# Two tiles a body, loaded row by row by SyncE, each with 25 of the empty places, and a new order of the first steps

## What is computed

```python
z = jnp.concatenate([x[dst], x[src], edge_attr], axis=-1)
msg = jax.nn.sigmoid(z @ Wf + bf) * jax.nn.softplus(z @ Ws + bs)
summed = jax.ops.segment_sum(msg, dst, num_segments=n)
cnt = jax.ops.segment_sum(jnp.ones((dst.shape[0],), x.dtype), dst, num_segments=n)
out = summed / jnp.maximum(cnt, 1.0)[:, None]
out = (out - rmean) * jax.lax.rsqrt(rvar + BN_EPS) * gamma + beta
return out + x
```

## Time and profile before

| | |
|---|---|
| median of the runs | 2086.69 us |
| the profiled execution | 2085.8 us, of which 2084.0 us span |
| busy: DVE, ACT, PE, POOL | 84%, 78%, 74%, 71% of the span |
| POOL's gathers, L402 | 1498 from the table, 56 of plain rows |
| SP's single rows, L330 | 1792 (14 tiles of 128) |
| mean TensorE clock granted | 0.94 of full |
| DMA | 339 MB, 163 GB/s in the mean |

### The profile page before, as it was taken

How to read it: one execution, slowest core, us unless ns; L and a number is a source line. 1 busy time by engine, 2 the same in 40 slices (tenths; PEclk the granted TensorE clock), 3 DMA queues, 4 the chain that set the end, 5 groups by cost and what they waited for, 6 DMA issues and landing times. The chain is left out here.

```text
span 2084.0 us, 41078 instructions
## 1 busy us (share of the span) xinstructions
PE 1540.8 (74%) x8321; PEld 1266.5 (61%) x8321; DVE 1745.7 (84%) x3574; ACT 1618.0 (78%) x3692; POOL 1481.8 (71%) x1575
## 2 busy tenths in 40 slices
PE   7777777777677777777587777777777777777773
PEld 6666666656556666565466566566665555666652
DVE  6799988989889889798638999798788887988887
ACT  5699887878778778688457889698787777877884
POOL 6577777777777777777267777777777777777770
PEclk9999999999999999999799999899899999999995
DMA  8455555555555555555475555555555555555552
GB/s 293 119 169 161 169 171 158 159 161 168 161 159 158 170 159 158 161 166 162 134 230 152 171 167 170 151 168 164 156 168 161 165 161 158 161 161 167 159 148 62
DMA packets 168890, 339.48 MB, mean 163 GB/s; under 512 B 62702, under 2 KB 93030, under 8 KB 168643
## 3 DMA queue, kind: packets, MB, share of 16 engines
q0 software_dynamic: 73824, 200.29, 32.4%
q1 hardware_dynamic: 93298, 135.27, 21.7%
q10 hardware_dynamic: 1522, 1.72, 0.3%
HBM read 315.49 MB, written 19.81 MB: 161 GB/s over the span
## 5 line engine op out<-in xcount | busy, mean ns | idle before, releaser
L402 POOL DMA_INDIRECT pre<-s_rows,ends x1498 | 1417.8, 946 | 482.9 <-issue 445.8
L516 PE MATMUL pre_ps<-rhs,lhs 128*128 128x256 f32 x3136 | 832.7, 409 | 450.5 <-DVE lhs L774 449.8
L516 PEld LDWEIGHTS pre_ps<-rhs,lhs 128*128 128x128 f32 x3136 | 592.6, 199 | 667.6 <-DVE lhs L774 418.8
L798 DVE TENSOR_TENSOR pre<-pre_ps,pre 128x1024 f32<-128x1024 f32 x378 | 460.6, 1219 | 50.5 <-DMA pre<-s_rows,ends 50.5
L609 ACT ACTIVATE logs<-pre 128x512 f32<-128x512 f32 x392 | 246.9, 630 | 306.6 <-DVE pre L798 265.9
L774 DVE SCALAR_TENSOR_TENSOR lhs<-lhs,base_f,sum_ps 64x256 f32<-64x256 int32 x784 | 373.3, 476 | 114.7 <-issue 51.8
L531 PEld LDWEIGHTS sum_ps<-hot,msg 128*128 128x128 f32 x3136 | 435.1, 201 | 55.9 <-issue 25.0
L531 PE MATMUL sum_ps<-hot,msg 128*128 128x64 f32 x3136 | 414.3, 278 | 29.6 <-DVE sums L817 19.4
L603 ACT COPY rhs<-dst_ps 64x256 f32<-64x256 f32 x792 | 290.0, 366 | 62.6 <-issue 31.3
L809 DVE TENSOR_TENSOR msg<-soft_ps,logs 128x512 f32<-128x512 f32 x392 | 271.0, 691 | 13.3
L802 DVE SCALAR_TENSOR_TENSOR soft_ps<-soft_ps,pre 128x512 f32<-128x512 f32 x392 | 270.4, 690 | 1.1 <-ACT soft_ps L616 1.0
(11 more groups left out here) (92 smaller groups left out, 573.7 us busy)
## 6 DMA issues: line engine op xcount, KB each, us to landing
lhs<-dge_and_destination_cols SPq DMA_DIRECT2D x196, 512.0 KB
single<-s_rows SPq DMA_DIRECT2D x1792, 1.0 KB
pre<-s_rows,ends POOLq DMA_INDIRECT x1498, 2.8
s_rows<-logs SPq DMA_DIRECT2D x8, 512.0 KB, 7.3
s_rows<-x_t SPq DMA_DIRECT2D x7, 512.0 KB, 12.0
s_rows<-msg SPq DMA_DIRECT2D x6, 512.0 KB, 7.0
x_rows<-pre SPq DMA_DIRECT2D x12, 256.0 KB
out<-y_out SPq DMA_DIRECT2D x12, 256.0 KB, 2.3
```

Of the source, the lines that this page charges most:

```text
L402: nc.gpsimd.indirect_dma_start(pre[:, slot(k, j), i, 0:width], None, rows, bass.IndirectOffsetOnAxis(ap=ends[:, k, j * TILES + i, 0:1], ax ...
L516: ins = nc.tensor.matmul(pre_ps[:, j % 2, i, :], lhs[:, j // 2, edges], rhs[:, j, i // 2, :], start=True, stop=not plain(b, k, j))
L798: nc.vector.tensor_tensor(rows, pre_ps[:, j % 2], rows, ALU.add).then_inc(s_pre[j], 1)
```

## The change

- `SINGLES = ((3, 3), (6, 3))`: two tiles a body, the last tiles of steps 15 and 27, are left to SP. Each of the 28 such tiles of the program (14 a layer) holds only 103 edges (`SINGLE_ROWS`): its last 25 places are empty. 14 x 25 = 350 of the 352 empty places are moved there from the end of the list, by the host's arrangement of the inputs.
- SP issues 206 single rows a body where it issued 128, in all 14 halves, 13 to 17 in each (7 in the last; `CUT`), where it was 12 in each of 11. `single` and `sp_src` have two places. The list of the first tile is read during the body before; that of the second in halves 1 and 3. The first tile is put in place at the start of half 7, after the last of its rows landed, the second at the end of half 13.
- POOL gathers 110 tiles a body where it gathered 111.
- Layer 1's stages come in another order: `hot`, `logs`, `msg`, then five in `x1_t`, of which stores 10 to 12 use the first three again. ACT waits for the flag of sortedness before double 10, not before the first.
- The four memsets of the counts go from DVE to POOL, ahead of its wait for the stores.
- DVE makes `one_hot` of steps 1 to 3 right after `hot_transposed`. PE's `turn` is called at the end of the step before.
- DVE clears `single` once a layer (the 25 empty rows are never written after).

```diff
-SINGLE = (BODY - 1, SLOTS - 1, TILES - 1)
-SINGLE_ROWS = 12
+SINGLES = ((3, 3), (6, 3))
+SINGLE_ROWS = 103
+CUT = ((0, 13, 30, 43, 60, 73, 90, 103), (0, 17, 32, 49, 64, 81, 96, 103))
...
-            s_stage = in_x1[0:3] + s_stage[0:2] + s_stage[4:5] + s_stage[2:4] + in_x1[3:5]
+            s_stage = s_stage[4:5] + s_stage[0:4] + in_x1
...
+        place = lambda c: (c if c < len(s_stage) else c - len(in_x1)) if first else c % len(s_stage)
+        stores_of = lambda r, c=STORES: 16 * sum(place(e) == r for e in range(c))
...
+            def load_singles(i, part):
+                rows = range(CUT[i][part], CUT[i][part + 1])
+                at_row = nc.values_load_multi_w_load_instructions(
+                    sp_src[:, i, rows[0]:rows[-1] + 1], engines=[ENG.SP], min_val=0, max_val=NPAD - 1,
+                    skip_runtime_bounds_check_because="sources are rows of the table")[1]
+                for p, r in zip(rows, at_row):
+                    sp.dma_start(single[p:p + 1, i, :], s_dram[bass.ds(r, 1), :]).then_inc(singles_in, 16)
+
+            def place_singles(i, b):
+                k, j = SINGLES[i]
+                sp.wait_ge(singles_in, b * (32 * SINGLE_ROWS) + (i + 1) * (16 * SINGLE_ROWS))
+                sp.sem_inc(passed, 1)
+                done(sp, s_soft, group_no(b, k), j, RING)
+                sp.sem_inc(passed, 1)
+                sp.dma_start(pre[:, slot(k, j), TILES - 1, :], single[:, i, :]).then_inc(single_in, 16)
+
+            def singles(b, half):
+                if half == 0:
+                    sp.wait_ge(list_in, b * 64 + 32)
...
+                if half == BODY:
+                    sp.wait_ge(list_in, b * 64 + 64)
+                    sp.sem_inc(passed, 1)
+                    place_singles(0, b)
+                load_singles(half // BODY, half % BODY)
+                if half == 1:
+                    load_block(group_no(b, SINGLES[1][0]))
+                if half == 3:
+                    load_list(1, b * 64 + 48)
+                if half == BODY + 2:
+                    load_block(group_no(b, SINGLES[0][0]) + BODY)
+                if half == BODY + 4:
+                    load_list(0, b * 64 + 80)
                 if half == 2 * BODY - 1:
-                    place_singles(b, group_no(b, SINGLE[0]))
+                    sp.wait_ge(single_in, b * 32 + 16)
+                    sp.sem_inc(passed, 1)
+                    place_singles(1, b)
...
+                        if first:
+                            for c in range(4):
+                                cols = slice(c * (NPAD // 4), (c + 1) * (NPAD // 4))
+                                nc.gpsimd.memset(t["sums"][:, 1, cols], 0.0).then_inc(zeroed, 1)
...
-                    gather(s_dram, F2, k, j, TILES - ((k, j) == SINGLE[0:2]))
+                    gather(s_dram, F2, k, j, TILES - ((k, j) in SINGLES))
...
-                    if plain(b, k, j):
-                        turn(SLOTS * k + j)
-                    else:
+                    if not plain(b, k, j):
                         product(b, k, j)
...
                     if plain(b, k, j):
                         product(b, k, j)
+                        if SLOTS * k + j + 1 < PLAIN:
+                            turn(SLOTS * k + j + 1)
...
-                if c >= len(s_stage) and i % 2 == 0:
-                    act.wait_ge(s_out[r], 16 * (c // len(s_stage)))
+                if stores_of(r, c) and i % 2 == 0:
+                    act.wait_ge(s_out[r], stores_of(r, c))
...
-                if live(0) and four_back:
+                if live(0) and (four_back or SLOTS * k + j):
                     one_hot(g, k, j)
```

More of the change, by code:

```diff
@@ L214, in store_rows @@
             sp.dma_start(dram[c * 4 * P:(c * 4 + n) * P, :].rearrange("(w p) f -> p w f", p=P),
-                         stage[c % len(stage)][:, 0:n, :]).then_inc(out[c % len(stage)], 16)
+                         stage[place(c)][:, 0:n, :]).then_inc(out[place(c)], 16)
         @block.sync
@@ L320, in load_singles @@
                         for r in range(len(s_stage)):
-                            sp.wait_ge(s_out[r], 16 * len(range(r, STORES, len(s_stage))))
+                            sp.wait_ge(s_out[r], stores_of(r))
                     else:
-                        sp.wait_ge(single_in, b * 16)
+                        sp.wait_ge(single_in, b * 32)
                         sp.sem_inc(passed, 1)
[L325 to L338, removed]
@@ L348, in one @@
+            load_block(SINGLES[0][0])
+            load_list(0, 16)
             def one(b, k):
@@ L373, in _ @@
             sp.wait_ge(sp_tab_in, groups * 16 + 16)
+            sp.wait_ge(list_in, bodies * 64 + 32)
             sp.sem_inc(passed, 1)
@@ L646, in one @@
                     step = SLOTS * k + j - 3
-                    if first and isinstance(b, int) and step in (0, 12):
-                        for r in ((0, 1, 2) if step == 0 else (8, 9)):
-                            act.wait_ge(s_out[r], stores_of(r))
+                    if first and isinstance(b, int) and step in range(0, 4 * len(in_x1), 4):
+                        act.wait_ge(s_out[5 + step // 4], stores_of(5 + step // 4))
                     if first and isinstance(b, int) and 0 <= step < DOUBLES:
@@ L789, in sums @@
                 done(v, s_prod, g, j, 0)
-                single = (k, j) == SINGLE[0:2]
-                v.wait_ge(src_in[k][j], turn * (16 * (TILES - single)))
-                if single:
-                    v.wait_ge(single_in, turn * 16)
+                if (k, j) in SINGLES:
+                    v.wait_ge(src_in[k][j], turn * (16 * (TILES - 1)))
+                    v.wait_ge(single_in, turn * 32 + 16 * (SINGLES.index((k, j)) - 1))
+                else:
+                    v.wait_ge(src_in[k][j], turn * (16 * TILES))
                 rows = pre[:, slot(k, j), :, 0:F2]
@@ L860, in stages @@
                 step = SLOTS * k + j
-                if first and isinstance(b, int) and step < 4:
-                    nc.vector.memset(t["sums"][:, 1, step * (NPAD // 4):(step + 1) * (NPAD // 4)], 0.0).then_inc(zeroed, 1)
                 if isinstance(b, int) and step == 0:
                     v.wait_ge(s_out[hot_stage], stores_of(hot_stage))
-                if live(0) and not four_back:
+                if live(0) and not four_back and step == 0:
                     one_hot(g, k, j)
@@ L1067 @@
     x_t[:, :NODES] = a["x"].T
-    dst = np.full((EPAD + P,), NO_NODE, a["dst"].dtype)
-    dst[:EDGES] = a["dst"]
+    short = np.array([(g * SLOTS + j) * TILES + TILES - 1 for g in range(GROUPS) for k, j in SINGLES if g % BODY == k])
+    used = np.ones((EPAD // P, P), bool)
+    used[short, SINGLE_ROWS:] = False
+    place = np.flatnonzero(used)[:EDGES]
+    last = np.arange(PAIR - 1, EPAD, PAIR)
+    last[short // (TILES // PAIRS)] -= P - SINGLE_ROWS
+    in_order = np.full((EPAD + P,), NO_NODE, a["dst"].dtype)
+    in_order[:EDGES] = a["dst"]
+    dst = np.full((EPAD,), NO_NODE, a["dst"].dtype)
+    dst[place] = a["dst"]
     ends = np.zeros((EPAD, 2), a["src"].dtype)
-    ends[:EDGES, 0] = a["src"]
-    ends[:, 1] = dst[:EPAD]
+    ends[place, 0] = a["src"]
+    ends[:, 1] = dst
     features = np.zeros((FE, EPAD), a["edge_attr_64"].dtype)
-    features[:, :EDGES] = a["edge_attr_64"].T
+    features[:, place] = a["edge_attr_64"].T
     features = features.reshape(FE, EPAD // STEP, PAIRS, PAIR)
-    ends_row = dst[:EPAD].view(features.dtype).reshape(EPAD // STEP, PAIRS, PAIR)
+    ends_row = dst.view(features.dtype).reshape(EPAD // STEP, PAIRS, PAIR)
     edge_cols = np.empty((P, EPAD // STEP, PAIRS, PAIR), features.dtype)
```

60 lines of the change are left out of this document (27 added, 33 removed).

## The result

The kernel became slower: 2432.7 us in the median of four runs (2429.81 to 2434.64) against 2086.3 for the kernel before beside it (2085.7 to 2089.22). The ratio is 1.1656, interval [1.1636, 1.1676]. The direction was as forecast, the size wasn't: 2172 us was forecast and 2225 was the top of the range. The rise is 346 us where 86 were expected, four times as much.

The account below looks back on a forecast made before the run. POOL was taken as the bound before the change, SyncE after: 100.1 + 32.4 + 5.2 + 2.3 + 0.8 + 2.7 = 143.5 us a body; 2084.0 + 45.4 + 40.9 plus 1.8 around gave 2172 us, range 2100 to 2225.

Parts of the forecast that it names:

- What bounds the kernel now: In the loop before the change, POOL sets the pace at 1.250 us a gather; SyncE has some 39 us to spare.
- POOL, 17.5 us: POOL's 7 fewer gathers a layer save 17.5 us; its body falls from 138.8 to 137.5 us.
- SyncE, more rows, 32.4 us a body: On SyncE's queue, 78 more rows a body at 0.415 us each add 32.4 us.
- SyncE, register reads, +5.2 us (bounds 0.9 to 9): SyncE's reads of row numbers into registers grow from 10.2 to 15.4 us a body, bounds 0.9 to 9 more.
- The second list and the placement, 2.3 and 0.8: On SyncE, loading a second list adds 2.3 us a body and placing a second tile 0.8.
- Waits for landing, 2.7 us a body (bounds 0 to 5): SyncE's two waits a body for the tiles' last rows to land add 2.7 us, bounds 0 and 5.
- First bodies: At layer starts, step 4's edge load issues at 68 us behind 30 rows; second bodies begin 16.2 and 8.5 us later.
- Ends of the layers: Last sums come at 1050.2 us in layer 1, +45.4, and 2073.6 us in layer 2, +40.9.
- Layer 1's new stages: PE's first step moves 12 us later to about 43.5; net 4 us later in layer 1, 3 to 4 earlier in layer 2.
- Who waits: In the loop, POOL's gathers wait for the softplus of 7 steps back, tens of us a layer; VectorE waits for `lhs`.
- Rival B: SyncE's rows cost more, reads cut in two and landing waits of 2.5 us each: 149.6 us a body, 2255 us; 4%.
- Rival C: TensorE's clock falls to 1.2 GHz through waits for edges at every half: body 157 us, 2340 us in all; 3%.

Follow-up runs that it names:

- 80 rows: The changed kernel issuing only 80 of each tile's 103 single rows, in parts of 12, so part of the computation is left out: 2070.93 us, ratio 0.9921.
- the last version: The changed kernel with aligned cuts, 24 rows on ScalarE, old stage order, fewer early rows in first bodies: 2067.79 us, ratio 0.9896; slow chip 3155.99 us, 1.0726.

## Why the prediction was wrong

By its own steps.

- **What bounds the kernel now**: right. POOL at 1.250 us a gather shows again as soon as SyncE has room (80 rows), and SyncE's spare 39 us swallowed reads that took some 17 us a body more (2.67 for 0.95 us nine times, 1.67 for 0.72 once).
- **POOL, 17.5 us**: near the size: 0.9921 with 80 rows is 16.5 us, of which 3 are the first steps', so 13.5 are left for it. In the changed kernel it is worth nothing, since POOL isn't the bound.
- **SyncE, more rows, 32.4 us a body**: right, 0.414 measured for 0.415.
- **SyncE, register reads, +5.2 us (bounds 0.9 to 9)**: this is the step that failed. The reads take 34.8 us a body, 24.6 more than before. The slope of 0.057 us a number came from reads of 8 and of 12 numbers, and both start at multiples of 12; the change moved the starts as well as the lengths, and no row of before has a read with such a start. So the bound from above (9) was drawn from a case of the trace that doesn't contain what the change does. With 34.8 for 15.4 the sum is 143.5 + 19.4 = 162.9, less 0.9 for the landings 162.0; 161.7 were measured. Over 14 bodies that is 14 x (161.7 - 143.5) = 255 us, and between the two spans lie 2428.0 - 2170.3 = 258. The one term is the whole miss.
- **What the Trainium skill says of it**: the page "Runtime: NRT & Kernel Launch" (Instruction fetch mechanics) gives about 200 ns a register, for the runtime's own loads from HBM; the reads here are from SBUF. For reads that start off a multiple of four, 0.28 + 0.2 us a number agree with it. For the others the measurement decides: 0.27 us and 0.225 for each four numbers, as 8, 12 and 16 take 0.72, 0.945 and 1.17. The prediction's "The trace disagrees" took the one kind of read that its trace had as a refutation of the figure; the body of "some 154 us" that it named beside the sum would have been nearer than its own.
- **The second list and the placement, 2.3 and 0.8**: not measured by themselves; the body's sum leaves 0.3 us for an error in them, unless errors cancel.
- **Waits for landing, 2.7 us a body (bounds 0 to 5)**: 2 x 0.88 = 1.8.
- **First bodies**: timeline of PE and of SyncE in the changed kernel, PE's first step and the edges of step 4:

```profile
42.13 1.20 PE L523 MATMUL dst_ps<-w_node,x_cols 128*128 128x256 f32 x2 [0.93 <-issue]
...
68.70 0.37 SPq L265 DMA_DIRECT2D lhs<-dge_and_destination_cols  x1
```

  They are at 42.1 for the 43.5 worked out, and at 68.7 for 68. The second body's first edge load, worked out at 186.7, goes out at 189.9 with the cuts at multiples of four, and at 201.6 with the dear reads.
- **Ends of the layers**: the last sums of the layers in VectorE's timeline, for the earlier trace rows:

```profile
1181.42 1.23 DVE L823 TENSOR_TENSOR pre<-pre_ps,pre 128x1024 f32<-128x1024 f32 x1
2376.64 1.23 DVE L823 TENSOR_TENSOR pre<-pre_ps,pre 128x1024 f32<-128x1024 f32 x1
```

  Layer 1 ends 1181.42 - 1004.78 = 176.6 us later (45.4 expected), layer 2 adds 344.0 - 176.6 = 167.4 (40.9). Both are off by nearly the same, 131 and 127, as one term that repeats in every body makes them.
- **Layer 1's new stages**: direction and size were right where they could be seen (PE's first step 10.7 us later for the 12 worked out, paid for by the one_hot and the memsets), and the net was 3 us of gain where the prediction had at most 1 of loss.
- **Who waits**: POOL was to wait for the softplus of seven steps back. It waited three times as long for `ends` (256.1 us against 83.4): SyncE's lateness hit POOL directly, before it came round by PE and VectorE. VectorE's wait for `lhs` came as told.
- **Rival B** (more dear reads) pointed at the right term, the reads, with another mechanism ("cut in two") and too small a size: 149.6 us a body. **Rival C**: the mechanism was there. The product of a step after a pause of 3.85 us takes 3.75 us, with a granted clock of 0.50 (1.2 GHz), and the one after 0.47 us takes 2.00, with 1.00 (2.4 GHz; PE's timeline):

```profile
718.67 3.75 PE L538 MATMUL pre_ps<-rhs,lhs 128*128 128x256 f32 x8 [3.85 <-DVE lhs L798]
...
730.54 2.00 PE L538 MATMUL pre_ps<-rhs,lhs 128*128 128x256 f32 x8 [0.47 <-DVE lhs L798]
```

  But it cost nothing in the loop: SyncE never waits for PE's products in this kernel, so a slower product can't lengthen SyncE's body. (The 2340 us of this rival count its 18 us a body from the time before; from the forecast, 13.5 us a body above 143.5, they would be 2361.)

The 208 us between the range's top and the result had one cause, and it lay in the numbers of `CUT`, which the prediction read for how many rows a part has and not for where it begins.

## What to carry to other kernels

When a change moves a cost measured in the trace to another size, ask what else moves with it (the start, the parity, the tile) and whether any row of before has that value; if none has, the bound from above must come from the dearest price that anything gives, and here the 200 ns a register of the Trainium skill ("Runtime: NRT & Kernel Launch", Instruction fetch mechanics) was one. Cut lists that a queue reads into registers at multiples of 16 bytes. A queue with slack hides such a defect completely, so the slack of the engine that will carry the added work is the first number to take, and each of its instructions, reads too, counts towards it; a few rows given to a second queue with time turned this change from 4.6% slower into 0.5% faster.

## What the runs showed of the hardware

- A register read (TENSOR_LOAD from a tile in SBUF) of 7 to 17 numbers on SyncE: where it starts at a multiple of 16 bytes, 0.27 us + 0.225 for each four numbers + 0.2 for each left over, to 0.05 us (measured 0.72 us for 8, 0.945 for 12, 1.16 for 13, 1.17 for 16, 1.40 for 17, 1.59 for 15, 1.14 for 7); elsewhere 0.28 + 0.2 us a number (1.67 for 7, 2.67 for 12, 2.88 for 13, 3.27 for 15, 3.67 for 17). An even start is not enough: the read of 13 from number 30 on takes 2.886 us. So 15 numbers cost more than 16.
- Outside this the rule doesn't hold. Reads of one number on SyncE take 0.28 us from one tile and 0.45 from another. On ScalarE reads of four take 0.31 us or 0.49: mostly the one from number 4 on is the dear one, but in the last version's first bodies it is the one from number 8 on (0.49 and 0.50), and that from 4 takes 0.31. So the start alone doesn't settle it there, and what does is open.
- The landing of the last single row, issued just before or with one edge load behind it, is awaited for 0.88 us in the mean and 1.5 at the most.
- One chip ran the unchanged kernel 40% slower than the others, with a granted clock of 0.80 (0.78 with the last version, whose trace has waits there that no instruction of the core ended). Only a comparison on the same chip is one.
